# Four chained attention blocks on eight images: the last image's fourth layer runs beside that of the image before

## The chip, the cores and the metric

The kernel runs on one core of a Trainium2 chip. The metric is the time of one execution on the device, in microseconds (us), as the median of several runs; lower is better. A profile is one further execution, taken by the hardware profiler.

## The reference

Eight images of 256 channels by 1024 positions (float32) go through four layers one after another.

```python
def reference(x, ...):
    x = _L0_conv_ref(x, ...)   # group norm, attention among the 32 channels of a head, residual
    x = _L1_conv_ref(x, ...)   # one head, 1024 x 1024 attention, residual
    x = _L2_conv_ref(x, ...)   # group norm, 8 heads, 1024 x 1024 attention, residual to x
    x = _L3_conv_ref(x, ...)   # the same, but the residual is the normalised x
    return x

def _L3_conv_ref(x, gamma, beta, w_qkv, w_out, b_out):
    xn = group_norm(x, gamma, beta)
    q, k, v = split(einsum('oc,bcn->bon', w_qkv, xn.reshape(b, c, n)), 3)
    sim = einsum('bhdi,bhdj->bhij', q * scale, k)          # 8 heads of 32 channels
    out = einsum('bhij,bhdj->bhid', softmax(sim), v)
    return (einsum('oc,bcn->bon', w_out, out) + b_out[None, :, None]).reshape(b, c, h, w) + xn
```

Images don't depend on one another; the layers of one image do. In the code the layers have the numbers 0 to 3, and the "fourth layer" is layer 3.

## The kernel before

**Groups.** The attention of layers 2 and 3 is cut into four *groups*: group g = 2 * t + qc takes the four heads of tile t (128 channels) and half of the queries (512). Below, "3,1" is layer 3, group 1. A group has eight steps of 128 keys. In a step PE makes four score tiles of 128 x 512, one for each head (line 1210), ACT takes their exponentials into one of four slots `prob` (line 853), PE multiplies them by the values (line 1232), and POOL adds the slots up to `acc`, seven additions of 128 x 2048 in a group (line 756). At the end PE sums `acc` over its partitions (`finish`, line 1253), DVE inverts the sums (lines 996 to 1000), ACT copies the values out of PSUM (`evacuate`, line 834), and POOL scales them into `att` (`scale`, line 734). A slot of `prob` is used again once PE and POOL have read it.

The exponentials need each query's maximum beforehand. So for every group there are 32 more score products (`max`, line 1181), of which DVE takes the maximum (line 972), a split of the maxima into two halves on DVE (lines 978 to 986), and a `maxrow` that PE, ACT and a DMA put as extra rows under the queries `Q` (lines 1188, 829, 682). A group's first score waits for that DMA.

**Pieces.** All else is cut into `side` pieces that share two banks of PSUM: the projection to queries and keys (`qk`, line 1132: PE, then ACT writes `hi`, DVE writes the rest `lo`, and three DMAs, a `stack`, copy both under each other into `Q` or `K`, line 670), the values (`v`, line 1140), the output projection (`out`, line 1156) and the mean of the normalisation. A normalisation is four `stats` and a `norm` on DVE, `mean` on PE and DVE (`gvar`, line 920), `power` on POOL (four small operations from line 715), and four `apply` on ACT (line 780), which write `ha` or `hb`.

**Order.** `group_sequence` lists by hand, for every *turn*, the groups in their order, and for each group its pieces with slots (32 slots a group, one for each score tile) and the maxima of later groups with their slots. `plans` makes of each turn one list of events, and every engine walks the same list and issues its part of each event, in order. The scores run one step ahead of the values (`LAG`). `gap(pieces)` lets all late values end, then issues its pieces one after another, and then the 32 maxima and the `maxrow` of the next group in a row.

There are five turns. The third, `steady`, is a hardware loop of six rounds. In a steady turn groups 2,1 to 2,3 of one image stand beside layer 0 of the next, then come 3,0 of the image before, layer 1 of the next image, 3,1 to 3,3 of the image before, and 2,0 of the next image. In 3,2 stand the early `qk` pieces of layer 2 (`early2`), in 3,3 its `v` pieces, in 2,0 the late `qk` pieces (`late2`) and the output of layer 3 (`out3`). The fourth turn, `last2`, has groups 2,1 to 2,3 of image 7 (the last, counted from 0) and 3,0 to 3,3 of image 6, and ends in a gap with `out3`. The fifth, `last3`, begins with a gap with the normalisation, the early `qk` pieces and the `v` pieces of layer 3 of image 7, has its four groups, and ends in a gap with `out3`.

**Places.** `images` and `normed` say from which tile a layer's image is read and into which it is normalised: layer 2 reads `xa` and writes `ha`, layer 3 reads `xb` and writes `hb`. `vT2` and `vT3` hold the values of layers 2 and 3. `Q`, `K`, `att`, `acc` and the maxima have one place each.

Of the kernel before, what the change touches and what calls it, by code (L numbers as in the profile page):

```python
# [8 lines left out]
ALU = mybir.AluOpType  # L9
# [4 lines left out]
B = 8  # L14
# [22 lines left out]
STEPS = {1: KC // HPT, 2: KC, 3: KC}  # L37
MAXIMA = {1: QT * NQ, 2: HPT * QT * NQ, 3: HPT * QT * NQ}
# [42 lines left out]
def side(layer, what, n):  # L81
    return [("side", layer, what, i) for i in range(n)]
# [37 lines left out]
def group_sequence():  # L120
    end = LAST_PIECE
    out2, out3 = side(2, "out", T * NQ), side(3, "out", T * NQ) + [("store",)]
# [12 lines left out]
    def rows(layer, g, slot):  # L135
        return (layer, g, None, None, slot, slot)
# [21 lines left out]
    def layer2_begins(pieces):  # L158
# [21 lines left out]
    end3 = [(3, 2, [], [(3, 3, 8, 32, 0, 23), rows(3, 3, 27)]), (3, 3, [], []), gap(out3)]  # L180
    last2 = (layer2(True, False)
             + [(3, 0, spread(0, 14, late3) + spread(SCALED, end, out2),
                 [(3, 1, 8, 32, 0, 23), rows(3, 1, 27), (3, 2, 0, 8, 24, 31)]),
                (3, 1, [], [(3, 2, 8, 32, 0, 23), rows(3, 2, 27), (3, 3, 0, 8, 24, 31)])] + end3)
    last3 = ([gap(normalise(3) + early3 + side(3, "v", KC // 2)),
              (3, 0, spread(0, 20, late3), [(3, 1, 0, 32, 0, 23), rows(3, 1, 27), (3, 2, 0, 8, 24, 31)]),
              (3, 1, [], [(3, 2, 8, 32, 0, 23), rows(3, 2, 27), (3, 3, 0, 8, 24, 31)])] + end3)
    return [first, second, steady, last2, last3]


RUNS = [1, 1, B - 2, 1, 1]
# [173 lines left out]
def build(nc, x, wqk0T, wv0, wp0T, rows0, waT1, woT1, wqkv2T, wp2T, wqkv3T, wp3T, cols, consts, scratch, out):  # L365
# [63 lines left out]
    with ctx:  # L429
# [30 lines left out]
        images = {0: xa, 2: xa, 3: xb}  # L460
        normed = {0: ha, 2: ha, 3: hb}
# [20 lines left out]
        vT = {1: vT1, 2: vT2, 3: vT3}  # L482
# [15 lines left out]
        maxpart[3] = maxpart[2]  # L498
# [120 lines left out]
        def _(sp):  # L619
# [10 lines left out]
            def program(b, number):  # L630
                for e in b.plan:
# [16 lines left out]
                    elif e[0] == "stack":  # L648
# [4 lines left out]
                        users = [] if layer == 1 else [(user, NQ * t + NQ - 1) for user in (2, 3)]  # L653
# [29 lines left out]
                    elif e[0] == "store":  # L683
                        sp.wait_ge(*taken(b, ("side", 3, "out", T * NQ - 1)))
                        sp.dma_start(image(out, number - 1), hb[:, :, :]).then_inc(stored, 16)
# [5 lines left out]
        def _(pool):  # L691
# [11 lines left out]
            def program(b, number):  # L703
                for e in b.plan:
                    if e[0] == "power":
                        pool.wait_ge(var_ready, b.after(NORMS, ("norm", e[1])))
                        layer = e[1]
                        steps = 6 if layer == 0 else 3
# [10 lines left out]
                        own(pool.tensor_tensor(ga[:, :], rstd[:, :], col(f"gn{layer}_scale"), ALU.mult), 2)  # L719
                        own(pool.tensor_tensor(shift[:, :], gm[:, :, 0], ga[:, :], ALU.mult), 3)  # L720
                        pool.tensor_tensor(gb[:, :], col(f"gn{layer}_bias"), shift[:, :],
# [583 lines left out]
```

## Time and profile before

| | us |
|---|---|
| median of 3 runs | 3344.45 (3338.95 to 3347.55) |
| the profiled execution's own time | 3339.21 |
| its span, from the first to the last instruction | 3337.3 |
| PE busy (matmul) | 2901.6 (87%) |
| POOL busy | 2336.4 (70%) |
| DVE busy | 1853.0 (56%) |
| ACT busy | 1553.8 (47%) |

PE is TensorE, DVE VectorE, ACT ScalarE, POOL GpSimd, SP the engine that issues the DMAs here. The span is divided into stretches by naming their bounds in us from its start; the clock is the share of TensorE's full clock of 2.4 GHz that was granted. "Idle before <- X" tells how long an engine stood idle ahead of an instruction, and what released it; "issue" means that it waited for nothing that the profile shows.

### The profile page before, as it was taken

To read this page: it belongs to the slowest core of one execution; us is meant where nothing else is said; L and a number is where in the kernel's file an instruction comes from. 1 tells how busy PE (TensorE), PEld (TensorE's weight loads), DVE (VectorE), ACT (ScalarE), POOL (GpSimd) and SP (SyncE) were. 2 spreads that over 40 slices of the span, in tenths; PEclk is the share of its full clock that TensorE was granted. 3 is DMA by queue.
4 is the path that set the end of the run, shared out by engine and by line. 5 is a ranking of instruction groups with operands and counts; after the bars stand their busy time and mean duration, and the time that the engine had idled before them with its cause. 6 is when DMAs were issued, how large, how long until landed. Compare 5 with 4: busy or idle time off the path is not lost.

```text
span 3337.3 us, 46964 instructions
## 1 busy us (share of the span) xinstructions
PE 2901.6 (87%) x12840; PEld 1431.4 (43%) x12840; DVE 1853.0 (56%) x3293; ACT 1553.8 (47%) x2794; POOL 2336.4 (70%) x781
## 2 busy tenths in 40 slices
PE   5678868999989998999989998999989999886686
PEld 3334334454445444554435444554445444432332
DVE  0255227556665666566664666566665667662461
ACT  1225323545554455545554455545554455553153
POOL 2228524868886787778876787778886788988087
PEclk8779877999999999999999999999999999998698
DMA  1150033331441334332440334332440334330320
GB/s 57 28 71 27 11 51 53 53 49 29 52 84 19 40 53 66 53 49 39 52 80 13 40 53 66 53 49 39 52 81 12 40 52 65 41 40 1 57 34 14
DMA packets 74159, 151.71 MB, mean 45 GB/s; under 512 B 9073, under 2 KB 10609, under 8 KB 73906
## 3 DMA queue, kind: packets, MB, share of 16 engines
q1 hardware_dynamic: 73906, 148.56, 28.9%
q8 instruction: 132, 2.16, 0.3%
q14 instruction: 121, 0.99, 0.1%
HBM read 20.46 MB, written 16.78 MB: 11 GB/s over the span
## 4 chain that ended last, share of the span: by engine, by line
PE 54%; POOL 14%; issue 13%; DMA 6%; DVE 5%; ACT 5%; SPq 1%; POOLq 0%; ACTq 0%; DVEq 0%
POOL acc L756 13%; PE psum L1210 12%; PE psum L1232 9%; PE psum L1181 9%; PE psum L1132 4%; PE psum L1156 4%; PE psum L1140 3%; DVE maxpart L972 3%; PE psum L1228 3%; DMA Q<-lo 3%; DMA K<-hi 3%; ACT prob L853 2%; PE psum L1253 2%; PE psum L1074 2%; ACT ha L780 1%
## 5 line engine op out<-in xcount | busy, mean ns | idle before, releaser
L756 POOL TENSOR_TENSOR acc<-acc,prob 128x2048 f32<-128x2048 f32 (+1 forms) x480 | 1870.0, 3896 | 202.9 <-ACT prob L853 171.6
L972 DVE TENSOR_REDUCE maxpart<-psum 128x1 f32<-128x512 f32 x2176 | 1404.1, 683 | 881.7 <-PE psum L1181 853.0
L853 ACT ACTIVATE prob<-psum 128x512 f32<-128x512 f32 x2176 | 1224.2, 596 | 1040.0 <-PE psum L1210 1003.8
L1210 PE MATMUL psum<-Q,K 104*128 104x512 f32 x2048 | 1080.8, 530 | 112.1 <-ACT prob L853 58.7
L1181 PE MATMUL psum<-K,Q 96*128 96x512 f32 x2048 | 860.4, 430 | 61.8 <-DMA K<-hi 49.6
L1210 PEld LDWEIGHTS psum<-Q,K 104*128 104x128 f32 x2048 | 396.0, 194 | 817.9 <-ACT prob L853 423.1
L756 POOL TENSOR_TENSOR acc<-prob 128x2048 f32<-128x2048 f32 (+1 forms) x80 | 312.2, 3903 | 601.7 <-ACT prob L853 316.3
L1232 PE MATMUL psum<-prob,vT 128*32 128x512 f32 x4096 | 581.7, 628 | 0.0
L1181 PEld LDWEIGHTS psum<-K,Q 96*128 96x128 f32 x2048 | 413.3, 202 | 216.7 <-issue 83.9
L1232 PEld LDWEIGHTS psum<-prob,vT 128*32 128x32 f32 x4096 | 102.2, 111 | 209.1 <-ACT prob L853 115.9
L1253 PE MATMUL psum<-acc,ones 128*32 128x512 f32 x640 | 93.6, 659 | 84.8 <-POOL acc L756 84.8
L996 DVE STREAM_TRANSPOSE turned_sums<-psum 128x512 f32<-128x512 f32 x80 | 56.5, 707 | 171.6 <-PE psum L1253 171.6
L1132 PE MATMUL psum<-ha,wqkv_sb 128*128 128x512 f32 x256 | 136.0, 626 | 14.6 <-ACT ha L780 14.6
L1132 PE MATMUL psum<-hb,wqkv_sb 128*128 128x512 f32 x256 | 139.8, 638 | 5.4 <-ACT hb L780 5.4
L1156 PE MATMUL psum<-att,wp_sb 128*128 128x512 f32 x256 | 132.3, 617 | 10.1 <-POOL att L734 10.1
L734 POOL TENSOR_TENSOR att<-att,turned_sums 128x512 f32<-128x512 f32 x80 | 102.0, 1275 | 46.1 <-DVE turned_sums L1000 46.1
L1228 PE MATMUL psum<-prob,products 128*128 128x512 f32 x256 | 116.8, 600 | 0.0
L829 ACT CAST max_rows<-psum 8x512 fp32r<-8x512 f32 (+1 forms) x80 | 46.2, 577 | 136.1 <-PE psum L1188 134.9
L940 DVE SCALAR_TENSOR_TENSOR lo<-psum,cols_sb,hi 128x512 fp32r<-128x512 f32 x64 | 48.0, 751 | 106.3 <-ACT hi L808 106.3
L715 POOL TENSOR_TENSOR rstd<-gvar,half_power 128x2 f32<-128x2 f32 x24 | 16.8, 698 | 125.6 <-DVE gvar L920 125.6
L834 ACT COPY att<-psum 128x512 f32<-128x512 f32 x80 | 46.9, 586 | 100.5 <-PE psum L1228 57.0
L940 DVE SCALAR_TENSOR_TENSOR lo<-psum,hi 128x512 fp32r<-128x512 f32 x64 | 44.1, 690 | 83.0 <-ACT hi L808 82.9
(110 smaller groups left out, 1969.6 us busy)
## 6 DMA issues: line engine op xcount, KB each, us to landing
Q<-hi SPq DMA_DIRECT2D x128, 256.0 KB
K<-hi SPq DMA_DIRECT2D x128, 256.0 KB
Q<-lo SPq DMA_DIRECT2D x64, 256.0 KB
K<-lo SPq DMA_DIRECT2D x64, 256.0 KB
xa<-in_x SPq DMA_DIRECT2D x8, 1024.0 KB, 8.4
scratch<-xa SPq DMA_DIRECT2D x8, 1024.0 KB, 4.1
xb<-scratch SPq DMA_DIRECT2D x8, 1024.0 KB, 4.9
out<-hb SPq DMA_DIRECT2D x8, 1024.0 KB, 5.4
```

The source lines that it names most:

```text
L734: pool.tensor_tensor(dst, dst, turned_sums[:, :, :].rearrange("p a c -> p (a c)"), ALU.mult).then_inc(group_done, 1)
L756: pool.tensor_tensor(total, first if a == 1 else total, this, ALU.add).then_inc(added, 1)
L853: act.activation(prob[STEP_STARTS.slot(b, start)][:, j, :], score_bank[(SCORES.rank[b.n][e] - 1) % SCORE_BANKS], ACT.Exp, scale=1.0 if lay ...
L972: dve.tensor_reduce(maxpart[layer][:, a // NQ, a % NQ:a % NQ + 1], bank, AX_X, ALU.max).then_inc(max_free, 1)
L1132: ins = pe.matmul(side_bank, wqkv_sb[layer][:, t, o:o + P], normed[layer][:, t, part], start=(t == 0), stop=(t == T - 1))
L1140: ins = pe.matmul(side_bank[:, a * width:(a + 1) * width], src[:, t, kt * P:(kt + 1) * P], w[:, t, o:o + width], start=(t == 0), stop=(t = ...
L1156: ins = pe.matmul(side_bank, w[:, t, ot * P:(ot + 1) * P], src[:, t, part], start=(t == 0), stop=(t == T - 1))
L1181: pe.matmul(max_bank[(r - 1) % MAX_BANKS], left, right, start=True, stop=True).then_inc(max_full, 1)
L1210: pe.matmul(score_bank[(r - 1) % SCORE_BANKS], left, right, start=True, stop=True).then_inc(score_full, 1)
L1228: ins = pe.matmul(values_bank, vT1[:, kt, :], slot[:, j, :], start=(kt == 0), stop=(kt == KC - 1))
L1232: ins = pe.matmul(values_bank[head_rows(j), :], vT[layer][:, s, head * DH:(head + 1) * DH], slot[:, j, :], start=(s == 0), stop=(s == KC - 1),
L1253: ins = pe.matmul(side_bank[head_rows(j), :], ones[:, :], acc[:, 0 if layer == 1 else j, :], start=(layer == 1 or POOLED == KC), stop=True ...
```

## The change

The two last turns are made one. Layer 3 of image 7 gets a number of its own, `LAST3 = 4`, and the names of its groups are 4,0 to 4,3 below. It is normalised into `ha` and has its values in `vT2`, the places of layer 2, and shares the weights, the maxima and `xb` with layer 3. Its normalisation stands in group 3,1 of image 6, its early `qk` pieces in 3,2, its `v` pieces in 3,3, and `late4` and the output of image 6 in 4,0. The maxima of group 4,0 stand in 3,2 and 3,3, those of 4,1 in 3,3 and 4,0. The two gaps between the images are left out; the last one stays. The turns before, and the new turn up to group 3,0, are as they were.

```diff
-STEPS = {1: KC // HPT, 2: KC, 3: KC}
-MAXIMA = {1: QT * NQ, 2: HPT * QT * NQ, 3: HPT * QT * NQ}
+LAST3 = 4
+STEPS = {1: KC // HPT, 2: KC, 3: KC, LAST3: KC}
+MAXIMA = {1: QT * NQ, 2: HPT * QT * NQ, 3: HPT * QT * NQ, LAST3: HPT * QT * NQ}
...
-    end3 = [(3, 2, [], [(3, 3, 8, 32, 0, 23), rows(3, 3, 27)]), (3, 3, [], []), gap(out3)]
-    last2 = (layer2(True, False)
-             + [(3, 0, spread(0, 14, late3) + spread(SCALED, end, out2),
-                 [(3, 1, 8, 32, 0, 23), rows(3, 1, 27), (3, 2, 0, 8, 24, 31)]),
-                (3, 1, [], [(3, 2, 8, 32, 0, 23), rows(3, 2, 27), (3, 3, 0, 8, 24, 31)])] + end3)
-    last3 = ([gap(normalise(3) + early3 + side(3, "v", KC // 2)),
-              (3, 0, spread(0, 20, late3), [(3, 1, 0, 32, 0, 23), rows(3, 1, 27), (3, 2, 0, 8, 24, 31)]),
-              (3, 1, [], [(3, 2, 8, 32, 0, 23), rows(3, 2, 27), (3, 3, 0, 8, 24, 31)])] + end3)
-    return [first, second, steady, last2, last3]
-
-
-RUNS = [1, 1, B - 2, 1, 1]
+    out4 = side(LAST3, "out", T * NQ) + [("store", LAST3)]
+    early4, late4 = (split_operand(LAST3, m) + split_operand(LAST3, m + 1) for m in (0, 2))
+    last = (layer2(True, False)
+            + [(3, 0, spread(0, 14, late3) + spread(SCALED, end, out2),
+                [(3, 1, 8, 32, 0, 23), rows(3, 1, 27), (3, 2, 0, 8, 24, 31)]),
+               (3, 1, at((1, 2, 3, 4, 5, 8, 11, 15, 16, 17, 18), normalise(LAST3)),
+                [(3, 2, 8, 32, 0, 23), rows(3, 2, 27), (3, 3, 0, 8, 24, 31)]),
+               (3, 2, spread(0, 20, early4), [(3, 3, 8, 32, 0, 23), rows(3, 3, 27), (LAST3, 0, 0, 8, 24, 31)]),
+               (3, 3, spread(0, end, side(LAST3, "v", KC // 2)),
+                [(LAST3, 0, 8, 32, 0, 23), rows(LAST3, 0, 27), (LAST3, 1, 0, 8, 24, 31)]),
+               (LAST3, 0, spread(0, 14, late4) + spread(SCALED, end, out3),
+                [(LAST3, 1, 8, 32, 0, 23), rows(LAST3, 1, 27), (LAST3, 2, 0, 8, 24, 31)]),
+               (LAST3, 1, [], [(LAST3, 2, 8, 32, 0, 23), rows(LAST3, 2, 27), (LAST3, 3, 0, 8, 24, 31)]),
+               (LAST3, 2, [], [(LAST3, 3, 8, 32, 0, 23), rows(LAST3, 3, 27)]), (LAST3, 3, [], []), gap(out4)])
+    return [first, second, steady, last]
+
+
+RUNS = [1, 1, B - 2, 1]
...
-        images = {0: xa, 2: xa, 3: xb}
-        normed = {0: ha, 2: ha, 3: hb}
+        images = {0: xa, 2: xa, 3: xb, LAST3: xb}
+        normed = {0: ha, 2: ha, 3: hb, LAST3: ha}
...
-        vT = {1: vT1, 2: vT2, 3: vT3}
+        vT = {1: vT1, 2: vT2, 3: vT3, LAST3: vT2}
...
-        maxpart[3] = maxpart[2]
+        maxpart[3] = maxpart[LAST3] = maxpart[2]
+        wp_sb[LAST3], wqkv_sb[LAST3] = wp_sb[3], wqkv_sb[3]
...
-                        users = [] if layer == 1 else [(user, NQ * t + NQ - 1) for user in (2, 3)]
+                        users = [] if layer == 1 else [(user, NQ * t + NQ - 1) for user in (2, 3, LAST3)]
...
-                        sp.wait_ge(*taken(b, ("side", 3, "out", T * NQ - 1)))
-                        sp.dma_start(image(out, number - 1), hb[:, :, :]).then_inc(stored, 16)
+                        sp.wait_ge(*taken(b, ("side", e[1], "out", T * NQ - 1)))
+                        sp.dma_start(image(out, number - 1 if e[1] == 3 else number),
+                                     normed[e[1]][:, :, :]).then_inc(stored, 16)
```

The rest of the diff lets the `power` event and the output of layer `LAST3` find their columns and their tile.

On POOL, from the additions of 3,2 of image 6 to the second group of image 7, the kernel before has (line 756 the additions, 734 the scaling, 715 to 721 the normalisation):

```order
L756 TENSOR_TENSOR acc<-prob 128x2048
L734 TENSOR_TENSOR att<-att,turned_sums 128x512
L756 TENSOR_TENSOR acc<-acc,prob 128x2048 x6
L734 TENSOR_TENSOR att<-att,turned_sums 128x512
L715 TENSOR_TENSOR rstd<-gvar,half_power 128x2
L719 TENSOR_TENSOR ga<-rstd,cols_sb 128x2
L720 TENSOR_TENSOR shift<-gm,ga 128x2
L721 TENSOR_TENSOR gb<-cols_sb,shift 128x2
L756 TENSOR_TENSOR acc<-prob 128x2048
L756 TENSOR_TENSOR acc<-acc,prob 128x2048 x6
```

The changed kernel has, on POOL, from the additions of 3,0 to those of 3,1 of image 6 (its line numbers are some ten higher: 765, 743, 724 to 730):

```order
L765 TENSOR_TENSOR acc<-prob 128x2048
L743 TENSOR_TENSOR att<-att,turned_sums 128x512
L765 TENSOR_TENSOR acc<-acc,prob 128x2048 x6
L724 TENSOR_TENSOR rstd<-gvar,half_power 128x2
L728 TENSOR_TENSOR ga<-rstd,cols_sb 128x2
L729 TENSOR_TENSOR shift<-gm,ga 128x2
L730 TENSOR_TENSOR gb<-cols_sb,shift 128x2
L765 TENSOR_TENSOR acc<-prob 128x2048
L743 TENSOR_TENSOR att<-att,turned_sums 128x512
L765 TENSOR_TENSOR acc<-acc,prob 128x2048 x6
```

The four small operations have moved from behind the last scaling of image 6, where POOL has nothing queued, to a place between the seventh addition of 3,0 and the first of 3,1.

On PE, at the same border, the kernel before has (1232 values, 1253 `finish`, 1156 `out`, 1049 `mean`, 1132 `qk`, 1140 `v`, 1181 maxima, 1188 `maxrow`, 1210 scores):

```order
L1232 MATMUL psum<-prob,vT 32x512 x8
L1253 MATMUL psum<-acc,ones 32x512 x4
L1156 MATMUL psum<-att,wp_sb 128x512 x8
L1049 MATMUL psum<-mv,const_sb 128x4
L1132 MATMUL psum<-hb,wqkv_sb 128x512 x8
L1140 MATMUL psum<-wqkv_sb,hb 128x256 x16
L1181 MATMUL psum<-K,Q 128x512 x32
L1188 MATMUL psum<-ident_bf,maxsplit 8x128 x4
L1210 MATMUL psum<-Q,K 128x512
```

The changed kernel has, on PE, in group 3,2 of image 6 (1142 `qk`, 1191 maxima, 1220 scores, 1242 values):

```order
L1220 MATMUL psum<-Q,K 128x512
L1191 MATMUL psum<-K,Q 128x512
L1142 MATMUL psum<-ha,wqkv_sb 128x512
L1242 MATMUL psum<-prob,vT 32x512 x4
L1220 MATMUL psum<-Q,K 128x512
L1191 MATMUL psum<-K,Q 128x512
L1220 MATMUL psum<-Q,K 128x512
L1191 MATMUL psum<-K,Q 128x512
L1142 MATMUL psum<-ha,wqkv_sb 128x512
```

The eight projections of the border stand one by one among the scores, the maxima and the values of a group of the other image.

## Rows read from the trace of the kernel before

**Rows 1.** The page: busy us (share of the span), and line 756 of the costliest groups.

```profile
PE 2901.6 (87%) x12840; PEld 1431.4 (43%) x12840; DVE 1853.0 (56%) x3293; ACT 1553.8 (47%) x2794; POOL 2336.4 (70%) x781
...
L756 POOL TENSOR_TENSOR acc<-acc,prob 128x2048 f32<-128x2048 f32 (+1 forms) x480 | 1870.0, 3896 | 202.9 <-ACT prob L853 171.6
```

**Rows 2.** Stretches, 3,0 of image 6 on: bounds, length, busy us, clock, DMA, GB/s.

```profile
2929.80:2968.40 38.60, 35.86 (x164) 16.27 (x160) 26.90 (x45) 19.91 (x36) 33.16 (x8) 1.00 0.52 62
2968.40:3004.50 36.10, 29.08 (x144) 12.30 (x140) 22.55 (x39) 18.48 (x34) 33.12 (x9) 0.93 0.02 2
3004.50:3041.80 37.30, 27.29 (x128) 10.05 (x124) 12.43 (x24) 18.47 (x34) 33.09 (x9) 0.87 0.02 3
3041.80:3075.40 33.60, 18.54 (x88) 5.53 (x80) 1.54 (x3) 13.65 (x25) 32.88 (x8) 0.86 0.00 0
3075.40:3169.70 94.30, 61.78 (x136) 31.70 (x136) 37.40 (x67) 14.28 (x24) 2.55 (x5) 0.68 0.34 50
3169.70:3210.60 40.90, 36.53 (x159) 16.74 (x162) 27.27 (x46) 21.16 (x37) 31.86 (x7) 0.92 0.55 69
3210.60:3246.70 36.10, 29.04 (x144) 12.30 (x140) 22.53 (x39) 18.47 (x34) 33.13 (x8) 0.93 0.02 2
3246.70:3283.80 37.10, 27.40 (x128) 10.09 (x124) 12.43 (x24) 18.48 (x34) 33.13 (x9) 0.87 0.02 2
3283.80:3317.40 33.60, 18.69 (x88) 5.52 (x80) 1.54 (x3) 13.65 (x25) 32.88 (x8) 0.86 0.00 1
3317.40:3337.30 19.90, 11.21 (x24) 3.96 (x24) 4.68 (x7) 0.00 (x0) 1.26 (x1) 0.75 0.13 53
```

The busy times stand in the order PE, PE's weight loads, DVE, ACT, POOL, here and in the next group, each with its instructions.

**Rows 3.** Stretches: 2,0; 3,2; 3,2; 3,3; 2,0 (steady turns); 2,1; 2,2; 2,3 (fourth).

```profile
2026.90:2079.00 52.10, 42.19 (x186) 19.12 (x178) 31.89 (x58) 22.98 (x42) 34.32 (x13) 0.90 0.52 88
...
2325.00:2365.20 40.20, 35.12 (x160) 17.26 (x156) 24.63 (x42) 20.65 (x37) 33.11 (x9) 0.92 0.53 67
...
2698.80:2738.20 39.40, 34.34 (x160) 16.86 (x156) 24.62 (x42) 20.51 (x37) 33.12 (x9) 0.91 0.54 68
2738.20:2775.50 37.30, 37.06 (x180) 19.64 (x176) 24.25 (x41) 21.70 (x39) 33.18 (x9) 1.00 0.19 25
...
2775.50:2818.30 42.80, 40.30 (x186) 17.99 (x178) 31.72 (x58) 22.82 (x42) 34.37 (x12) 1.00 0.56 81
2818.30:2853.90 35.60, 29.79 (x136) 13.22 (x136) 23.05 (x39) 21.36 (x37) 33.10 (x9) 0.98 0.51 82
2853.90:2891.20 37.30, 32.68 (x156) 15.20 (x152) 23.25 (x40) 19.62 (x36) 33.17 (x9) 0.91 0.31 39
2891.20:2929.80 38.60, 38.29 (x180) 19.99 (x176) 24.27 (x41) 21.76 (x39) 33.16 (x8) 0.97 0.18 25
```

**Rows 4.** The chain of waits between the images: start us, us, what.

```profile
3109.24 11.25 DMA Q<-lo
...
3123.23 9.75 DMA K<-hi
...
3133.92 19.23 DVE maxpart L972 x32
```

**Rows 5.** POOL in order of time: start us, us, instruction, [idle before <- releaser].

```profile
2816.84 0.70 POOL L715 TENSOR_TENSOR rstd<-gvar,half_power 128x2 f32<-128x2 f32 x1 [5.85 <-DVE gvar L920]
...
2818.31 4.57 POOL L756 TENSOR_TENSOR acc<-prob 128x2048 f32<-128x2048 f32 x1
...
2968.41 4.58 POOL L756 TENSOR_TENSOR acc<-prob 128x2048 f32<-128x2048 f32 x1 [2.96 <-PE psum L1253]
```

**Rows 6.** ACT in order of time: the first exponentials of 2,1 and of 3,1.

```profile
2807.21 2.27 ACT L853 ACTIVATE prob<-psum 128x512 f32<-128x512 f32 x4 [1.66 <-PE psum L1210]
...
2961.94 2.27 ACT L853 ACTIVATE prob<-psum 128x512 f32<-128x512 f32 x4 [1.14 <-PE psum L1210]
```

**Rows 7.** PE in order of time: the loop's border, and 3,2 in a steady turn.

```profile
2065.70 0.76 PE L1210 MATMUL psum<-Q,K 104*128 104x512 f32 x1 [8.19 <-issue]
...
2721.52 0.79 PE L1181 MATMUL psum<-K,Q 96*128 96x512 f32 x1 [4.72 <-DMA K<-hi]
```

More of the change, by code:

```diff
@@ L121, in group_sequence @@
     end = LAST_PIECE
-    out2, out3 = side(2, "out", T * NQ), side(3, "out", T * NQ) + [("store",)]
+    out2, out3 = side(2, "out", T * NQ), side(3, "out", T * NQ) + [("store", 3)]
     out1 = after_layer1(False)
@@ L707, in program @@
                         layer = e[1]
-                        steps = 6 if layer == 0 else 3
+                        gn, steps = min(layer, 3), 6 if layer == 0 else 3
                         def own(ins, step):
@@ L718, in program @@
                             pool.wait_ge(h_ready, b.after(NORMS, ("norm", layer), 1))
-                        own(pool.tensor_tensor(ga[:, :], rstd[:, :], col(f"gn{layer}_scale"), ALU.mult), 2)
+                        own(pool.tensor_tensor(ga[:, :], rstd[:, :], col(f"gn{gn}_scale"), ALU.mult), 2)
                         own(pool.tensor_tensor(shift[:, :], gm[:, :, 0], ga[:, :], ALU.mult), 3)
-                        pool.tensor_tensor(gb[:, :], col(f"gn{layer}_bias"), shift[:, :],
+                        pool.tensor_tensor(gb[:, :], col(f"gn{gn}_bias"), shift[:, :],
                                            ALU.subtract).then_inc(affine_ready, 1)
@@ L773, in program @@
                         if layer == 3 and first:
-                            left = b.last(STORES, [("store",)], e)
+                            left = b.last(STORES, [("store", 3)], e)
                             if left is not None:
@@ L962, in program @@
                             else:
-                                ins = dve.scalar_tensor_tensor(hb[:, t, part], side_bank, col("proj3_b", t),
-                                                               hb[:, t, part], ALU.add, ALU.add)
+                                image3 = normed[layer][:, t, part]
+                                ins = dve.scalar_tensor_tensor(image3, side_bank, col("proj3_b", t), image3,
+                                                               ALU.add, ALU.add)
                             ins.then_inc(side_free, 1)
```

## The prediction

> **What bounds the kernel now.** I read the busy shares of the page first. PE is busy for 87% of the span and POOL for 70%, and neither share says which of them sets the pace; what POOL does is nearly all line 756, the additions of probability tiles [rows 1]. The change touches only the end of the program, so the next view is the table of stretches over the last 407.5 us, cut at the first addition of each attention group [rows 2]. Seven additions and one scaling fill 33.1 us of POOL in each group, whatever else runs. The groups 3,1 of both images take 36.1 us with PE busy for 29 of them, and 3,2 takes 37.1 to 37.3 with PE busy for 27: POOL and its hand-over to the next group bound these. Where weight products ride along (groups with `qk` or `v` pieces), PE is busy for 34 to 40 us of 37 to 43, and PE and POOL bound about equally [rows 2, 3].
>
> The stretch that matters is 3075.4 to 3169.7: 94.3 us in which POOL works 2.55 us [rows 2]. It is the border between the last two turns: image 6 drains, then image 7 is normalised, projected, its queries and keys are stacked by DMA, and its first 32 maxima are taken, all one after another. In the chain of waits there one stacking DMA stands with 11.25 us, the next with 9.75 us, and the 32 maxima on DVE with 19.23 us [rows 4]. A normal group has none of these bare.
>
> **The change, part by part.** Every turn before the last two is the same, and so is the last one up to group 3,0 of image 6, which begins its additions at 2929.8. I compare from there. Before, the eight groups of images 6 and 7 and the drain take 38.6 + 36.1 + 37.3 + 33.6 + 94.3 + 40.9 + 36.1 + 37.1 + 33.6 + 19.9 = 407.5 us [rows 2]. After, each group has a twin that the trace of before already shows, because the new turn hangs the pieces where the steady turn hangs those of the second layer.
>
> (a) *Group 3,0.* Nothing in it changes, but POOL's next addition now stands behind the four small operations of the normalisation (line 715 on), which wait for DVE's variance. The twin is the border between group 2,0 and the first group of the last turn but one: the exponentials of the new group begin at 2807.21, POOL is idle 5.85 us for `gvar`, and the first addition starts at 2818.31, so 11.1 us after the first exponential [rows 5, 6]. In 3,0 the next group's exponentials begin at 2961.94 and its first addition starts 6.5 us later, at 2968.41 [rows 5, 6]. The added wait is 11.1 - 6.5 = 4.6 us: 43.2 instead of 38.6. The four statistics on DVE, the mean on PE and the four `apply` on ACT are in the twin as well. Bounds: 38.6 if PE's lead hides the wait, 52.1 from the widest such border, that of the loop [rows 3].
>
> (b) *Group 3,1 with the normalisation.* The twin is the next stretch, 2818.3 to 2853.9: 35.6 us, with a reload and half of a projection besides, which 3,1 doesn't get [rows 3]. I take 35.6; the other end is 37.3.
>
> (c) *Groups 3,2 and 3,3.* They take the early `qk` pieces (four, each with three stacking DMAs) and the four `v` pieces. On SP's queue the DMAs wait for the last score of 3,1, and the `maxrow` DMA of 3,3 is queued behind them; PE waits for that one before its first score of 3,3. In the steady turn the same two groups, with the same maxima at the same slots, take 40.2 or 39.4 us and 37.3 us [rows 3]; what costs more than 36.1 there is PE waiting 4.72 us for the last key DMA [rows 7]. In the last turn but one, groups 2,2 and 2,3 with like pieces take 37.3 and 38.6, and there PE enters with a longer lead over POOL, as it will here. The pairs sum to 76.7 and 75.9; I take 76.3. Bounds: twice 36.1, and 40.2 + 38.6. Here lies the price of the cover: PE is busy 37.06 of 37.3 us in the `v` group, so no more can be hidden there.
>
> (d) *Group 4,0* is group 3,0 with another layer's output beside it: 38.6 us [rows 2], for the 40.9 of before. In the steady turn the same slots end in a normalisation and take 42.8 [rows 3]; here none follows. Bounds 36.1 and 42.8. The store of image 6 is issued behind the `maxrow` DMA of that group and ahead of the next one, which is due some 30 us later, so nobody waits.
>
> (e) *Groups 4,1, 4,2, 4,3 and the drain* are those of before: 36.1 + 37.1 + 33.6 + 19.9 = 126.7 us [rows 2]. The final output goes from `ha` instead of `hb`, of the same size.
>
> The border is gone and leaves only the short hand-over that ends every group, which the periods contain. Their sum is 43.2 + 35.6 + 76.3 + 38.6 + 126.7 = 320.4 us. The gain is 407.5 - 320.4 = 87.1 us, the span 3337.3 - 87.1 = 3250.2 us, and with the 1.9 us that lie around the span 3252.1. The profiled execution (3339.2) lies near the fastest of the three runs; from their median of 3344.45 the same gain leads to 3344.45 - 87.1 = 3257.4. I take the middle, **3255 us**, 2.7% below the median of before. A run can't tell less than about 0.3% from no change.
>
> **What the notes say against it.** DVE works 37.4 us in the border, with POOL idle [rows 2]; after the change all of it runs beside POOL's additions. In the trace POOL needs 33.12 us for a group with DVE busy 22.55 us, and 32.88 with DVE busy 1.54 [rows 2], so that company costs 0.24 us at most. The Trainium skill ("SBUF — State Buffer", SBUF: two separate sides) says that VectorE and GpSimd share a pair of ports under an exclusive lock, for VectorE operations in a two-port mode or with two SBUF inputs. Taken for all of the moved work it would give back up to 37 us and end near 3292; the trace speaks against it, since the maxima that make up most of it leave POOL's time as it was.
>
> At the loop's border PE stands still for 8.19 us with nothing to wait for that the profile shows [rows 7], and the stretch there takes 52.1 us, 9.3 more than the same stretch on the way out of the loop, 42.8 [rows 3]. The Trainium skill ("Runtime: NRT & Kernel Launch", Instruction fetch mechanics) says that a taken branch makes the sequencer fetch code before it goes on. By that rule the new seam, which has no branch, costs 43.2 and not 52.1; no run here has shown the merged code yet.
>
> **The rivals.**
> *The seam costs as at the loop.* If fetching code, or the order variance, mean, power, first addition, holds PE at the new seam as at the loop's border, 52.1 stands for 43.2: 3264. For it: five of the six ends of a steady turn are wide ones, of which this is the widest. Against: those five have the branch, and the sixth, with 42.8, hasn't [rows 3].
> *The operands' DMAs don't hide.* Each of the four early pieces may bare its DMA as in the border, where two show 11.25 and 9.75 us [rows 4]: about 21 us bare instead of the 4.72 that the steady turn shows [rows 7], so 3255 + 16 = 3271. Against: six steady turns with the same places.
> *Better than the twins.* POOL's floor of 36.1 holds for 3,2, 3,3 and 4,0 and the variance wait hides: 4.6 + 4.1 + 2.5 less, 3244.
> *It doesn't overlap as it says.* A reused place (`ha`, `vT2`, `maxpart`) or an in-order wait makes image 7 wait for the drain of image 6 after all: near 3340. Against: the last reader of `ha` and `vT2` is layer 2 of image 7, over by 2929.8.
> *Slower.* PE without a rest loses the granted clock. In the last 407 us the clock shown is 0.86 to 1.00 in the groups and 0.68 in the border [rows 2]. If the merged stretch ran at 1.2 GHz, PE's busy time would about double, from 36 to 72 us in each of the three groups with pieces (3,2, 3,3, 4,0) and from 29 to 58 in two others (3,1, 4,1), where it would pass POOL's 36: 3 x 34 + 2 x 22 = 146 us more, against 87 gained, and 3255 + 146 = 3401. It decides once six tenths of that stretch (87 of 146) run at the low level. Against: the stretches with the busiest PE show 1.00, the idle ones 0.86 [rows 2, 3].
>
> **How the numbers follow.** The forecast (3247 to 3262) 0.70; seam as at the loop (3264) 0.10; DMAs bare (3271) 0.07; better (3244) 0.05; the port lock (up to 3292) 0.02; no overlap (3340) 0.03; slower 0.03. The bounds of (a) to (d) give 4.6 + 4.1 + 2.5 = 11 us down, and 8.9 + 1.7 + 2.5 + 4.2 = 17 us up, so 3244 to 3272; I widen the ends by 1 to 2 us for the spread of the runs: 3243 to 3274, which leaves out the last three cases. Faster by over 0.3%: all but the last two cases, 0.94; within 0.3%: 0.03; slower: 0.03.
>
> **What would show it.** Each group's additions should follow the last group's with no hole over 10 us, and POOL's longest wait from 2930 on should be the one for `gvar`, 5 to 6 us, just before 2973. The first additions should start near 2973, 3009, 3047, 3085, 3124, 3160 and 3197, and the last 53.5 us look as before. The step on (c) is wrong if 3,2 and 3,3 sum to over 79; the step on (a) if its wait is over 8 us or PE shows an idle time without a releaser there; the whole view is wrong if POOL is idle for over 10 us anywhere before the drain, or if the granted clock falls under 0.8 in a group that carries pieces.

## The result, and the profile after

| | before | after |
|---|---|---|
| median | 3341.7 us (3331.81 to 3347.55, 4 runs) | 3262.3 us (3251.68 to 3265.28, 4 runs) |
| the profiled execution's own time | 3339.21 us | 3260.68 us |
| its span | 3337.3 us | 3258.8 us |
| PE busy | 2901.6 us (87%) | 2871.9 us (88%) |
| POOL busy | 2336.4 us (70%) | 2337.5 us (72%) |

The changed kernel is faster: the ratio of its time to that of before is 0.976, with a 95% interval of 0.9726 to 0.9793. It takes 79.4 us less by the medians and 78.5 us less by the spans of the two profiled executions. The forecast was 3255 us, within 3243 to 3274; the measured time is 7.3 us above it.

The busy shares of the page have hardly moved. POOL does the same work in a shorter span.

```profile
PE 2871.9 (88%) x12840; PEld 1422.2 (44%) x12840; DVE 1855.8 (57%) x3293; ACT 1556.8 (48%) x2794; POOL 2337.5 (72%) x781
```

The table of stretches answers to [rows 2]: one row for each group, from the first addition of 3,0 of image 6 to the end, in the trace of the changed kernel. The columns are the bounds, the length, the busy us of PE, PE's weight loads, DVE, ACT and POOL with their instructions, the granted clock, and the share and GB/s of the DMAs.

```profile
2932.90:2977.80 44.90, 41.92 (x186) 18.87 (x178) 31.62 (x58) 22.99 (x42) 34.37 (x12) 0.96 0.45 53
2977.80:3013.90 36.10, 28.48 (x132) 12.49 (x132) 22.11 (x38) 20.69 (x36) 33.14 (x10) 0.94 0.34 45
3013.90:3055.10 41.20, 36.02 (x160) 17.54 (x156) 24.17 (x41) 20.59 (x37) 33.02 (x8) 0.88 0.32 42
3055.10:3092.40 37.30, 37.00 (x180) 19.62 (x176) 24.29 (x41) 21.73 (x39) 33.18 (x8) 1.00 0.19 25
3092.40:3131.90 39.50, 35.98 (x164) 16.27 (x160) 26.92 (x45) 19.97 (x36) 33.19 (x9) 1.00 0.59 88
3131.90:3168.00 36.10, 29.03 (x144) 12.32 (x140) 22.56 (x39) 18.48 (x34) 33.14 (x8) 0.94 0.02 2
3168.00:3205.20 37.20, 27.45 (x128) 10.17 (x124) 12.44 (x24) 18.53 (x34) 33.12 (x9) 0.87 0.02 2
3205.20:3238.80 33.60, 18.73 (x88) 5.53 (x80) 1.53 (x3) 13.65 (x25) 32.85 (x8) 0.86 0.00 1
3238.80:3258.80 20.00, 11.28 (x24) 4.05 (x24) 4.68 (x7) 0.00 (x0) 1.26 (x1) 0.75 0.13 52
```

The row of 94.3 us in which POOL worked 2.55 us is gone. Every row but the last has 33 to 34 us of POOL in it, and the last three attention groups and the drain are those of before to 0.1 us. The nine rows take 325.9 us where ten took 407.5 [rows 2], so 81.6 us went in this part; the forecast said 87.1.

What POOL and PE wait for in the new rows, taken from the views of the two engines in order of time (start us, busy us, engine, line, instruction, and in brackets the idle time ahead of it and what ended it):

```profile
2976.34 0.70 POOL L724 TENSOR_TENSOR rstd<-gvar,half_power 128x2 f32<-128x2 f32 x1 [6.12 <-DVE gvar L929]
...
2977.82 4.57 POOL L765 TENSOR_TENSOR acc<-prob 128x2048 f32<-128x2048 f32 x1
...
3037.84 0.76 PE L1191 MATMUL psum<-K,Q 96*128 96x512 f32 x1 [4.66 <-DMA K<-hi]
...
3055.14 4.58 POOL L765 TENSOR_TENSOR acc<-prob 128x2048 f32<-128x2048 f32 x1 [4.01 <-PE psum L1263]
```

POOL's longest wait ahead of the drain is the 6.12 us for the variance (5.85 us in its twin [rows 5]), and PE waits 4.66 us for the last key DMA in 3,2 (4.72 us in the twin [rows 7]). Both waits came over with the pieces.

### The profile page after: what moved, and what is told of

Same layout as the page of the kernel before. It is cut to its first block, busy times and chain, and to the rows that moved or that the text cites. A ratio compares the mean times of both kernels' runs of the same rounds, so it can differ in the third digit from the quotient of the medians.

```text
span 3258.8 us, 46964 instructions
## 1 busy us (share of the span) xinstructions
PE 2871.9 (88%) x12840; PEld 1422.2 (44%) x12840; DVE 1855.8 (57%) x3293; ACT 1556.8 (48%) x2794; POOL 2337.5 (72%) x781
## 4 chain that ended last, share of the span: by engine, by line
PE 58%; POOL 11%; issue 11%; DMA 7%; DVE 6%; ACT 5%; SPq 1%; POOLq 0%; ACTq 0%; DVEq 0%
PE psum L1220 13%; PE psum L1242 10%; POOL acc L765 10%; PE psum L1191 9%; PE psum L1166 5%; PE psum L1142 4%; PE psum L1150 4%; DMA Q<-lo 4%; PE psum L1238 3%; DVE maxpart L982 3%; DMA K<-hi 3%; ACT prob L862 2%; PE psum L1263 2%; PE psum L1084 2%; ACT ha L789 1%
## 5 line engine op out<-in xcount | busy, mean ns | idle before, releaser
L1242 PE MATMUL psum<-prob,vT 128*32 128x512 f32 x4096 | 583.6, 630 | 0.0
L1142 PE MATMUL psum<-ha,wqkv_sb 128*128 128x512 f32 x288 | 152.8, 624 | 14.6 <-ACT ha L789 14.6
L1142 PE MATMUL psum<-hb,wqkv_sb 128*128 128x512 f32 x224 | 117.9, 613 | 0.0
L1150 PE MATMUL psum<-wqkv_sb,ha 128*128 128x256 f32 x288 | 79.2, 408 | 16.5 <-DVEq L952 16.5
```

Of the source, the lines that this page charges most:

```text
L1142: ins = pe.matmul(side_bank, wqkv_sb[layer][:, t, o:o + P], normed[layer][:, t, part], start=(t == 0), stop=(t == T - 1))
L1150: ins = pe.matmul(side_bank[:, a * width:(a + 1) * width], src[:, t, kt * P:(kt + 1) * P], w[:, t, o:o + width], start=(t == 0), stop=(t = ...
L1242: ins = pe.matmul(values_bank[head_rows(j), :], vT[layer][:, s, head * DH:(head + 1) * DH], slot[:, j, :], start=(s == 0), stop=(s == KC - 1),
```

## The experiments

Each ran once with a profile, and four of them in five runs for a median. Since single executions differ by several us ahead of the last turn, I compare the stretch from the first addition of 3,0 to the end: 407.5 us before, 325.9 us in the changed kernel.

**The border put back.** One turn, the new names and places, but everything of the border in a row again.

```diff
-               (3, 1, at((1, 2, 3, 4, 5, 8, 11, 15, 16, 17, 18), normalise(LAST3)),
+               (3, 1, [],
...
-               (3, 2, spread(0, 20, early4), [(3, 3, 8, 32, 0, 23), rows(3, 3, 27), (LAST3, 0, 0, 8, 24, 31)]),
-               (3, 3, spread(0, end, side(LAST3, "v", KC // 2)),
-                [(LAST3, 0, 8, 32, 0, 23), rows(LAST3, 0, 27), (LAST3, 1, 0, 8, 24, 31)]),
-               (LAST3, 0, spread(0, 14, late4) + spread(SCALED, end, out3),
-                [(LAST3, 1, 8, 32, 0, 23), rows(LAST3, 1, 27), (LAST3, 2, 0, 8, 24, 31)]),
+               (3, 2, [], [(3, 3, 8, 32, 0, 23), rows(3, 3, 27)]),
+               (3, 3, [], []), gap(out3 + normalise(LAST3) + early4 + side(LAST3, "v", KC // 2)),
+               (LAST3, 0, spread(0, 20, late4),
+                [(LAST3, 1, 0, 32, 0, 23), rows(LAST3, 1, 27), (LAST3, 2, 0, 8, 24, 31)]),
```

> The changed kernel with its one last turn, its names and its places, but with the border of before in it: the output of image 6, the normalisation, the early projections, the values and the first 32 maxima of image 7 stand one after another between 3,3 and 4,0. Theory (the gain is overlap): POOL idles about 92 us there again, 4,0 takes 40.9 us, and the time is that of before, 3330 to 3348 us. Rival (one turn and places of its own save something by themselves): under 3325 us.

It took 3334.02 us in one execution, and 407.5 us from 3,0 on, as before. Its row for the border:

```profile
3070.20:3164.50 94.30, 61.92 (x136) 31.75 (x136) 37.42 (x67) 14.29 (x24) 2.55 (x7) 0.68 0.34 50
```

The 94.30 us and 2.55 us of POOL are those of [rows 2]. So neither the single turn nor the places save anything by themselves; they only allow the overlap.

**Only the maxima left in the border.** The normalisation, the early projections and the values stand beside image 6; the first 32 maxima of image 7 follow the drain and the output.

```diff
-               (3, 2, spread(0, 20, early4), [(3, 3, 8, 32, 0, 23), rows(3, 3, 27), (LAST3, 0, 0, 8, 24, 31)]),
-               (3, 3, spread(0, end, side(LAST3, "v", KC // 2)),
-                [(LAST3, 0, 8, 32, 0, 23), rows(LAST3, 0, 27), (LAST3, 1, 0, 8, 24, 31)]),
-               (LAST3, 0, spread(0, 14, late4) + spread(SCALED, end, out3),
-                [(LAST3, 1, 8, 32, 0, 23), rows(LAST3, 1, 27), (LAST3, 2, 0, 8, 24, 31)]),
+               (3, 2, spread(0, 20, early4), [(3, 3, 8, 32, 0, 23), rows(3, 3, 27)]),
+               (3, 3, spread(0, end, side(LAST3, "v", KC // 2)), []), gap(out3),
+               (LAST3, 0, spread(0, 20, late4),
+                [(LAST3, 1, 0, 32, 0, 23), rows(LAST3, 1, 27), (LAST3, 2, 0, 8, 24, 31)]),
```

> The changed kernel, but only the normalisation, the early projections and the values of image 7 stand beside image 6; its first 32 maxima still follow the drain and the output of image 6. Theory (each bare step of the border costs what the chain of before shows): the border is 15.4 us for the drain and the output plus 36.7 us from the maxima to the first addition, 52 us instead of 94.3, and 3,2 is some 3 us shorter without the eight maxima that wait for the key DMA. Against the changed kernel 44 to 48 us more: 3299 to 3310 us. Rival (the projections and DMAs are what matters, and maxima in a row cost little): under 3280 us.

It took 3293.97 us, and 370.0 us from 3,0 on: 44.1 us more than the changed kernel, as expected of that stretch; the whole time is 5 us under the expected range, since 3,0 began at 2922.2 us in this run and at 2932.9 in the changed kernel. Its rows for 3,2 and for the border:

```profile
3003.10:3040.30 37.20, 31.38 (x144) 13.45 (x140) 13.80 (x26) 20.26 (x37) 33.07 (x8) 0.91 0.36 46
...
3074.00:3125.00 51.00, 39.31 (x86) 18.23 (x86) 31.33 (x54) 5.71 (x10) 1.26 (x1) 0.67 0.11 30
```

The border is 51.0 us (52 expected). So of the 94.3 us, 43 were the normalisation, the projections and their DMAs, and 51 the drain, the output, the maxima and the first steps of the next group. And 3,2 takes 37.2 us with the same projections and DMAs, but without the eight maxima that need the new keys: 4 us less than the 41.2 of the changed kernel. 3,3, which has the `v` pieces but no maxima here, takes 33.7 us instead of 37.3. So what takes 51 us bare costs the changed kernel some 8 us beside 3,2 and 3,3, and the difference is nearly all of the 44.

**The power behind the first addition.**

```diff
-               (3, 1, at((1, 2, 3, 4, 5, 8, 11, 15, 16, 17, 18), normalise(LAST3)),
+               (3, 1, at((1, 2, 3, 4, 5, 8, 12, 15, 16, 17, 18), normalise(LAST3)),
```

> The changed kernel with the power event of the last normalisation one slot later (12 for 11), so that POOL's four small operations stand behind the first addition and the scaling. Theory (their wait for the variance is what lengthens 3,0): the first addition of 3,1 starts 6.5 us after the group's first exponential instead of 11.1, and 3,0 takes 40 to 41 us instead of 44.9; the sum of 3,0 and 3,1 falls by 3 to 5 us. Rival (PE or ACT set the pace there, the later apply holds ACT): 3,1 gives it back and the sum of the two stays within 1 us of 80.9.

It took 3252.87 us. 3,0 took 41.9 and 3,1 37.6 us, 79.5 together instead of 80.9: neither of the two expectations, since 1.4 us is less than the 3 to 5 of the theory and more than the 1 of the rival. The first addition starts 8.1 us after the first exponential, not 6.5. On ACT and POOL in order of time:

```profile
2965.84 0.66 ACT L826 ACTIVATE mv<-mv 128x1 f32<-128x1 f32 x2 [1.92 <-DVE mv L903]
```

```profile
2967.55 4.58 POOL L765 TENSOR_TENSOR acc<-prob 128x2048 f32<-128x2048 f32 x1 [4.62 <-ACT prob L862]
```

A second wait had stood behind the first. In slot 5 ACT waits 1.92 us for the moments and does its part of `norm`, ahead of two exponentials that the first addition needs. And the four small operations, 1.5 us, have only moved into 3,1. From 3,0 to the end this run took 325.4 us, just 0.5 less than the changed kernel: 3,2 was 1.1 us shorter, but 4,0 took 40.9 us at a granted clock of 0.96, for 39.5 at 1.00.

**The whole normalisation later.**

```diff
-               (3, 1, at((1, 2, 3, 4, 5, 8, 11, 15, 16, 17, 18), normalise(LAST3)),
+               (3, 1, at((1, 2, 3, 4, 8, 11, 14, 18, 19, 20, 21), normalise(LAST3)),
```

> The changed kernel with the last normalisation later in group 3,1: norm in slot 8, mean 11, power 14, apply 18 to 21, instead of 5, 8, 11 and 15 to 18. The run with only the power behind the first addition lost ACT's wait of 1.9 us for the moments ahead of that addition. Theory (both waits stand ahead of the first addition, and both leave): the first addition of 3,1 starts 6.5 us after the first exponential, POOL's idle time before it is about 3 us, and 3,0 with 3,1 take 76 to 78.5 us instead of 79.4 to 80.9. Rival (PE or ACT give it back in 3,1): the sum is 79 us or more.

It took 3250.01 us; 3,0 and 3,1 took 40.5 and 37.9 us, 78.4 together. On POOL in order of time:

```profile
2966.51 4.55 POOL L765 TENSOR_TENSOR acc<-prob 128x2048 f32<-128x2048 f32 x1 [3.22 <-PE psum L1263]
...
2972.68 0.70 POOL L724 TENSOR_TENSOR rstd<-gvar,half_power 128x2 f32<-128x2 f32 x1 [0.29 <-DVE gvar L929]
```

The wait ahead of the first addition is 3.22 us, the wait for the variance 0.29, and ACT's wait for the moments 0.47 instead of 1.92. So both waits are all but gone, as the theory had it, and 3,0 and 3,1 take 2.5 us less than the 80.9 of the changed kernel. The granted clock of 3,0 is 0.96 in both. From 3,0 to the end this run took 322.2 us.

**Maxima later in 3,2.**

```diff
-               (3, 2, spread(0, 20, early4), [(3, 3, 8, 32, 0, 23), rows(3, 3, 27), (LAST3, 0, 0, 8, 24, 31)]),
+               (3, 2, spread(0, 20, early4), [(3, 3, 8, 32, 0, 23), rows(3, 3, 27), (LAST3, 0, 0, 8, 28, 31)]),
```

> The changed kernel with the first eight maxima of 4,0 in slots 28 to 31 of group 3,2 instead of 24 to 31. Theory (3,2 takes 41.3 us because PE, at slot 24, waits 4.7 us for the last key DMA): the wait falls under 2 us and 3,2 with 3,3 take 75 to 76.5 us instead of 78.6. Rival (the wait is only where PE shows its slack; POOL's prob slots set the pace): the wait moves or goes, and the sum of 3,2 and 3,3 stays within 0.7 us of 78.6.

It took 3249.57 us. PE's wait for the key DMA in 3,2 fell from 4.66 to 1.34 us. This wait, and the rows of 3,2 and 3,3:

```profile
3028.46 0.70 PE L1191 MATMUL psum<-K,Q 96*128 96x512 f32 x2 [1.34 <-DMA K<-hi]
...
3005.10:3043.70 38.60, 36.11 (x160) 17.22 (x156) 23.98 (x41) 20.64 (x37) 33.15 (x8) 0.90 0.35 45
3043.70:3081.00 37.30, 37.01 (x180) 19.63 (x176) 24.29 (x41) 21.71 (x39) 33.16 (x8) 1.00 0.18 25
```

75.9 us instead of 78.6. The theory holds, and the rival, that the wait was only slack, falls. From 3,0 to the end it took 321.9 us, but 1.6 us of what that is under 325.9 lie in 3,0, ahead of the edit.

**Pieces sooner in 3,2.** The other way to the same end.

```diff
-               (3, 2, spread(0, 20, early4), [(3, 3, 8, 32, 0, 23), rows(3, 3, 27), (LAST3, 0, 0, 8, 24, 31)]),
+               (3, 2, spread(0, 12, early4), [(3, 3, 8, 32, 0, 23), rows(3, 3, 27), (LAST3, 0, 0, 8, 24, 31)]),
```

> The changed kernel with the four early projections of image 7 spread over slots 0 to 12 of group 3,2 instead of 0 to 20, and the maxima of 4,0 from slot 24 as in the changed kernel. Theory (slot 24 comes before the last key DMA has landed): PE's wait for it falls from 4.7 to under 1.5 us and 3,2 with 3,3 take 75 to 77 us instead of 78.6. Rival (closer pieces make ACT wait for the DMAs of the piece before, as in the groups 3,0 and 4,0): ACT waits 3 us and more for the query DMAs within 3,2, and the sum stays at 78 us or more.

It took 3260.93 us. PE shows no wait for the keys in 3,2, and 3,2 and 3,3 take 37.3 and 38.7 us: 76.0 together, as the theory had it. ACT's wait for a query DMA came as the rival said, 3.9 us for a piece of 3,2, but the sum didn't suffer. The whole time shows nothing of it: 4,0 took 40.9 us at a granted clock of 0.96, so that the stretch from 3,0 to the end is 325.2 us, and the steady turns began at 583.6 us, against 579.6 in the run with later maxima. A gain of 2.6 us can be read from the periods of the groups, not from one time.

**The changed kernel again.** No edit, five executions and a second trace.

> The changed kernel once more, unaltered, for a second trace and more runs. Theory (the forecast was 7 us short because that profile came with a late start of 4 us and a long form of group 3,0, both of which vary from run to run): from the first addition of 3,0 to the end 322 to 326 us, as 325.9 in the first trace, and a median of 3252 to 3264 us. Rival (325.9 is the fixed length): 325.5 to 326.3 again.

The median was 3256.46 us (3256.04 to 3260.49), with a ratio to before of 0.9747 (0.9732 to 0.9762). The second trace took 325.8 us from 3,0 on, with the same periods as the first to 0.1 us. So the rival held for these two traces. Yet the kernel with later maxima, whose code is the same up to 3,2, took 43.3 us for 3,0 where these two took 44.9 and 44.8. The granted clock is what differs; the rows of 3,0, first of that kernel:

```profile
2925.80:2969.10 43.30, 40.28 (x186) 18.00 (x178) 31.65 (x58) 22.85 (x42) 34.43 (x13) 1.00 0.46 55
```

then of the changed kernel's second trace:

```profile
2932.90:2977.70 44.80, 41.83 (x186) 18.87 (x178) 31.60 (x58) 22.93 (x42) 34.34 (x12) 0.96 0.45 53
```

**Both edits in all turns.** The last turn has the later normalisation and the later maxima of the two runs above. In `layer2` the normalisation of layer 3 moves in the same way, and that of layer 0, in the same group, makes room; in the steady turn's 3,2 the maxima start at slot 28.

```diff
-            a += [(0, ("load",))] + at((10, 12, 14, 16, 17, 20, 23), normalise(0))
+            a += [(0, ("load",))] + at((10, 12, 14, 16, 19, 22, 25), normalise(0))
...
-            a += at((1, 2, 3, 4, 5, 8, 11, 15, 16, 17, 18), normalise(3))
+            a += at((1, 2, 3, 4, 8, 11, 14, 18, 19, 20, 21), normalise(3))
...
-                 (3, 2, spread(0, 20, early2), [(3, 3, 8, 32, 0, 23), rows(3, 3, 27), (2, 0, 0, 8, 24, 31)]),
+                 (3, 2, spread(0, 20, early2), [(3, 3, 8, 32, 0, 23), rows(3, 3, 27), (2, 0, 0, 8, 28, 31)]),
...
```

> The changed kernel with both edits in all turns: the fourth layer's normalisation later (8, 11, 14, 18 to 21), the one of layer 0 in the same group at 19, 22 and 25, and the first eight maxima of the next image in slots 28 to 31 of 3,2. Theory (POOL's first addition and PE's slot 24 wait in every steady turn as in the last): 3 to 6 us less in 2,0 and 2,1, and 1.5 to 2.7 us less in 3,2 and 3,3, of each of seven turns, 3220 to 3240 us, a ratio to before of 0.964 to 0.970. Rival (the group 2,2 with layer 0 is bound by PE and takes it back): 3250 us or more.

The median was 3234.11 us (3230.73 to 3235.27) and the ratio to before 0.9678 (0.9662 to 0.9693), against 0.9747 for the changed kernel in the same comparison. It beats both kernels and lies in the expected range. The gain didn't come as expected, though. Against the trace of before, in the mean of four steady turns, 3,2 took 36.7 us instead of 39.9 (and 3,3 37.3 as ever), but 2,0 and 2,1 together took 89.9 instead of 88.1. The same mean is 87.5 to 88.8 us in the eleven other traces, so the later normalisation costs something there. In one steady turn, 3,2 and then 2,1 of the changed kernel,

```profile
1951.60:1990.80 39.20, 34.18 (x160) 16.88 (x156) 24.68 (x42) 20.55 (x37) 33.10 (x8) 0.91 0.54 69
1707.00:1744.30 37.30, 31.95 (x138) 14.05 (x138) 25.67 (x48) 24.50 (x43) 34.97 (x16) 0.95 0.41 74
```

and of this one:

```profile
1949.80:1986.10 36.30, 33.97 (x160) 16.98 (x156) 24.38 (x42) 20.52 (x37) 33.08 (x8) 0.95 0.59 74
1699.00:1742.30 43.30, 38.51 (x160) 16.47 (x156) 27.74 (x56) 27.35 (x49) 36.25 (x20) 0.88 0.32 59
```

The same work takes 2.9 us less in 3,2. In 2,1 the later slots bring 8 more instructions on DVE, 6 on ACT and 4 on POOL into the group, whose first addition now stands ahead of them. So most of the 6 us only changed sides: the 2,0 before it took 47.1 us instead of 52.1, and the two together 90.4 instead of 89.3.

**The same without the steady turn's normalisations.** As the last one, with the slots of `layer2` put back.

> The changed kernel with the maxima of the next image in slots 28 to 31 of 3,2 in all turns, and the normalisation later only in the last turn; the steady turn's normalisations are where they were. In the run with both edits in all turns, 3,2 fell by 3.2 us in each steady turn, while 2,0 and 2,1 together rose by 1.7. Theory (in the steady turn the later normalisation costs and the maxima pay): 2,0 and 2,1 take 88 us again, 3,2 36 to 37.5, and the median is 3222 to 3234 us, at or below that run's 3234. Rival (the gain of 3,2 is given back in the groups after it, and the later normalisation paid elsewhere in the turn): 3236 us or more.

The median was 3239.76 us (3228.73 to 3243.47), a ratio of 0.9697 (0.9674 to 0.9719) to a before that was 3335.52 us in this comparison. 2,0 and 2,1 took 88.2 us again, as expected, but 3,2 took 38.0 us instead of 36 to 37.5, and the median missed its range: it lies where the rival had put it, at 3236 us or more. By the intervals it can't be told from the run before it.

**The maxima alone, in all turns.**

> The changed kernel with the maxima in slots 28 to 31 of 3,2 in all turns and nothing else. Theory: six steady turns give 2.5 to 3.2 us each and the last 2.7, so 18 to 22 us less than the changed kernel, 3235 to 3240 us, and 2 to 4 us above the run that also moves the last normalisation. Rival (PE-bound groups behind 3,2 take the gain): 3250 us or more.

3242.82 us (3236.43 to 3244.55), a ratio of 0.9716 (0.9698 to 0.9734), with 3,2 at 36.9 us in the mean of the same four turns. Against the changed kernel's 0.9747 that is 0.3% or 10 us, half of what I expected, and between theory and rival. The sum of the groups 2,0 to 2,2 varies from turn to turn and from run to run by 3 us and more, so a single turn can't tell how much of the gain of 3,2 is given back there. The whole stretch from the first steady turn to 3,0 of the last one can. It took 2342.9 to 2349.7 us in the nine traces with the maxima at slot 24, 2345.8 in the mean, and 2332.2 here, 13.6 us less. The six 3,2 in it took 15.4 us less than in the mean of the nine. So most of the gain stays, some 2.3 us for each turn and not the 2.5 to 3.2 of my expectation; the last turn adds 3.4 us (322.5 from 3,0 on). This trace is of the fastest of the five executions, and the median shows less.

In the run with both edits the same stretch took 2334.3 us, 2.1 more than here, but the last turn from 3,0 on 318.2 us, 4.3 less. Its ratio lies below this one's, and the intervals don't touch. So what the later normalisation gives by these two traces it gives in the last turn.

## Why the prediction was right

The time lies in the range, 7.3 us above the forecast, and the mechanism is shown: with the border put back, the 94.3 us and all of the 407.5 are back. By its own steps:

- **What bounds it.** Right. POOL is busy for 33 us of each group, and from 3,0 on it has no hole over 7 us ahead of the drain. With the border nothing else went.
- **The part up to 3,0**, which I took as unchanged, came 3.1 us later (2932.9 for 2929.8), in code that is the same. Two traces of the changed kernel start their steady turn at 587.1 and 587.0 us, one with later maxima at 579.6. Part of it is the clock, shown below. It isn't an effect of the change, but I had put only 1 to 2 us into the range for it. With (a) and (c) it made all the first additions late that the prediction names: the first two by 5 us, the others by 7 to 8 (3205.2 for 3197 at the last).
- **(a) The wait for the variance.** Forecast 43.2 us, measured 44.9, of which the wait is 6.12 us, and 43.3 in the kernel whose PE kept its full clock through 3,0. The term was right for that case; the rest is 1.6 us at the low level of the clock. It was incomplete: behind the wait on POOL stood ACT's for the moments, as two experiments showed.
- **(b)** 35.6 forecast, 36.0 measured.
- **(c) 3,2 and 3,3** is the term that was mis-sized: 76.3 us forecast, 78.6 measured (the rows of the table, from rounded bounds, give 41.20 + 37.30). I had taken the mean of a pair that shows the wait for the key DMA, 76.7, and of one that has PE's longer lead over POOL, 75.9. The lead was there: the first exponential of 3,2 stood 16 us ahead of its first addition. But it doesn't reach the stall. PE can be four steps ahead of POOL at most, and it had spent them before the key pieces in the second half of the group, which then go at POOL's pace. In the issues on SP's queue, in order of time (us of issue, us in the queue), the query pieces of 3,2 leave 12 and 7 us ahead of the group's first addition at 3013.9, the key pieces 9 us behind it:

```profile
3001.66 1.25 SPq L678 DMA_DIRECT2D Q<-hi  x2
...
3006.91 1.20 SPq L678 DMA_DIRECT2D Q<-hi  x2
...
3023.07 0.55 SPq L678 DMA_DIRECT2D K<-hi  x1
```

  Seven slots behind the last key piece stand the maxima that need its DMA. PE waited 4.66 us whatever the lead had been. Two ways of getting those maxima and that DMA apart gave 2.7 and 2.6 us back, and leaving them out of 3,2 gave 4.

  But the twin of 76.7 us had the same wait, so the wait explains only 0.4 of the 2.3 us. The other 1.9 lie in 3,2 (41.3 us for 39.4), and there the lead did harm. PE had spent its four steps early and rested 6.43 us before it could sum `acc` of 3,1; from 3011.8 to 3015.3 its granted clock was 0.50, and these eight products took 1.94 us, where the twin's took 1.06. DVE inverted the sums later for it, and POOL stood 1.28 us between its first addition and the scaling:

```profile
3011.75 1.94 PE L1263 MATMUL psum<-acc,ones 128*32 128x512 f32 x8 [6.43 <-POOL acc L765]
...
3019.68 1.27 POOL L743 TENSOR_TENSOR att<-att,turned_sums 128x512 f32<-128x512 f32 x1 [1.28 <-DVE turned_sums L1010]
```

  In the twin, in the trace of before, PE summed without a rest, at a clock of 1.00, and POOL didn't wait for the scaling:

```profile
2697.61 1.06 PE L1253 MATMUL psum<-acc,ones 128*32 128x512 f32 x8
...
2703.33 1.28 POOL L734 TENSOR_TENSOR att<-att,turned_sums 128x512 f32<-128x512 f32 x1
```

  The choice of the twin mattered too: the six steady turns of before show 39.1 to 40.2 us for 3,2, 39.9 in the mean, which makes a pair of 77.2. The last 0.6 us stand behind the wait for the keys, in POOL's waits for ACT and for PE. No run was made for this part. In the two runs that moved the power and the normalisation, PE waited 4.7 us for the keys as before, but POOL only 0.47 and 0.79 us for the scaling, and 3,2 took 40.1 and 40.5 us.
- **(d)** 38.6 forecast, 39.4 measured. Six traces show 4,0 with a granted clock of 1.00 and 39.3 to 39.5 us, three with 0.96 and 40.9. **(e)** 126.7 forecast, 126.9 measured.

The misses are 3.1 + 1.7 + 0.4 + 2.3 + 0.8 + 0.2 = 8.5 us, and the profiled execution (3260.7) lies 8.6 us above the sum made for it (3252.1). All six have the same sign, so no error hid another. The median of the second comparison, 3256.5 us, is 1.5 us off the forecast; that it is so near owes something to the 2.9 us that the middle between two starting values had added to the sum, and to luck.

**The rivals.** *The seam costs as at the loop:* no. At the new seam PE shows no idle time without a releaser, where the five borders of the loop show 4.7 to 8.6 us of it in the same trace; the next exponential came 1.15 us after the last, and 44.9 isn't 52.1. *DMAs that don't hide:* one of them shows, with the 4.66 us of its twin; the stretch stayed under my 79 us by 0.4. *The port lock:* POOL took 33.02 us for 3,2 with DVE busy for 24.17 us and 32.85 for 4,3 with 1.53, so again 0.2 us at most; the Trainium skill's rule ("SBUF — State Buffer", SBUF: two separate sides) names operations in a two-port mode or with two SBUF inputs, and the trace shows no cost of it for the reductions from PSUM that are most of DVE's work here. *Better than the twins:* no; the wait for the variance showed, and 3,2 and 3,3 took 78.6 us where 72.2 were the floor. *No overlap* and *slower:* no; the granted clock in the merged groups was 0.88 to 1.00.

## What to carry to other kernels

To price a stretch of work that is moved beside other work, look for its twin: a place in the trace where the same instructions already stand in the same order. Here the sum of twins came within 2% of a stretch of 326 us, and the waits of the twins came over to 0.3 us, so a twin's stall should be counted whole, not discounted for a lead that the buffers between the engines can't carry. Look also at how the engine enters the twin: here a longer lead ended in a rest, and the stretch behind the rest was 1.9 us longer than the twin with the same stall. Where a wait ahead of a queue is taken away, look for the next one in line before counting its length as gain: of the 4.6 us on POOL, 1.4 came back from the first edit and 2.5 only once ACT's wait had been moved too.

## What the runs showed of the hardware

The executions of the changed kernel lie up to 14 us apart (3251.7 to 3265.3). A part of that can be seen. In the first turn, in code that all these kernels share, the rows of 70 to 80 us read, in the changed kernel and in the one with later maxima:

```profile
70.00:80.00 10.00, 9.23 (x17) 4.32 (x16) 1.50 (x2) 0.59 (x1) 0.00 (x0) 0.61 0.00 0
```

```profile
70.00:80.00 10.00, 8.33 (x19) 3.63 (x20) 3.00 (x4) 0.59 (x1) 0.00 (x0) 0.98 0.00 0
```

In one PE was granted 0.61 of its full clock, in the other 0.98, after the same stretch at 0.50 with PE busy for 7.6 us of ten in both. The first addition of the program came at 110.1 us in the one and at 105.5 in the other. The same happened in 3,0, where the changed kernel's PE had a granted clock of 0.51 for 3.3 us, from 2944.9 on; that is the lower of its two levels, 1.2 GHz. These are two products of that stretch, and the like ones of before, where the clock hadn't fallen:

```profile
2945.29 0.63 PE L1191 MATMUL psum<-K,Q 96*128 96x512 f32 x1
2945.71 1.91 PE L1166 MATMUL psum<-att,wp_sb 128*128 128x512 f32 x2
```

```profile
2943.79 0.40 PE L1181 MATMUL psum<-K,Q 96*128 96x512 f32 x1
2944.03 1.02 PE L1156 MATMUL psum<-att,wp_sb 128*128 128x512 f32 x2
```

Two projections took 1.91 us instead of 1.02. In both kernels ACT had waited some 3.6 and then 1.6 us for the query DMAs, and PE for ACT, just before. Whether PE falls to the low level after so short a rest differs between executions of the same code: of the twelve traces 3,0 has a clock of 1.00 in three and 0.96 in nine, and in the same code the higher one goes with 1.6 us less (43.3 for 44.9). Two of the three are the traces without a normalisation beside 3,1 (before, and the border put back), so chance alone may not be all of it. Why it falls in one and not in the other, these runs don't tell.
